# One wait for two tiles: how SyncE issues the count-matrix writes of a graph kernel

## The reference, cut to what matters

```python
h = jnp.maximum(_layernorm(x, axis=-1), 0.0)
x = x + _L0_gnn_ref(h, edge_attr_64, ..., edge_index)   # an MLP for each edge, segment_sum over src
h = jnp.maximum(_layernorm(x, axis=-1), 0.0)
x = x + _L1_gnn_ref(h, W, attn, rel_emb, src, dst, edge_type_100)   # attention, segment_sum over dst
...
x = x + _L2_gnn_ref(h, edge_index, W, b)                # graph convolution, segment_sum(msg, col)
x = x + _L3_gnn_ref(h, edge_index, ...)                 # mean over the neighbours, segment_sum(x[src], dst)
```

## Time and profile before

| | |
|---|---|
| median of 3 runs | 3380.41 us (3377.36 to 3380.56) |
| the profiled execution | 3380.8 us, of which its span in the trace is 3379.1 us |
| mean granted TensorE clock over the span | 0.866 of full speed |
| edge tiles, first to last accumulation | 1330.8 to 2585.7 us from the span's start |
| busy over the span | PE 74%, DVE 77%, POOL 58%, ACT 44% |

### The profile page before, as it was taken

How to read it: one execution, slowest core, us unless ns; L and a number is a source line. 1 busy time by engine, 2 the same in 40 slices (tenths; PEclk the granted TensorE clock), 3 DMA queues, 4 the chain that set the end, 5 groups by cost and what they waited for, 6 DMA issues and landing times. The chain is left out here.

```text
span 3379.1 us, 87741 instructions
## 1 busy us (share of the span) xinstructions
PE 2511.1 (74%) x20390; PEld 1974.6 (58%) x20391; DVE 2597.0 (77%) x8325; ACT 1489.4 (44%) x3942; POOL 1952.3 (58%) x2344
## 2 busy tenths in 40 slices
PE   1433555555555554999999999999999239989899
PEld 1322334333334343999999999999997214445455
DVE  7863777777777773999999999999997779983501
ACT  2011222222222222677777777777775655452200
POOL 1005777777777777899999999999996000000000
PEclk9975677677777776999999999999999559999999
DMA  9993222222222223888888888888886669869766
GB/s 381 414 414 129 78 78 83 78 78 78 77 79 78 78 68 104 236 240 234 242 239 235 240 239 234 242 238 236 241 239 226 255 282 343 301 219 315 249 220 208
DMA packets 738172, 696.84 MB, mean 206 GB/s; under 512 B 48524, under 2 KB 637275, under 8 KB 734779
## 3 DMA queue, kind: packets, MB, share of 16 engines
q1 hardware_dynamic: 516770, 536.77, 47.6%
q10 hardware_dynamic: 195544, 104.71, 12.7%
q0 software_dynamic: 25792, 54.52, 4.9%
HBM read 340.91 MB, written 354.90 MB: 206 GB/s over the span
## 5 line engine op out<-in xcount | busy, mean ns | idle before, releaser
L855 POOL DMA_INDIRECT sorted_rows<-rows,posi x806 | 785.1, 974 | 338.7 <-issue 221.4
L1147 DVE SCALAR_TENSOR_TENSOR acc<-acc,keep,pm 128x256 f32<-128x256 f32 x1504 | 715.7, 476 | 70.9 <-issue 23.9
L965 POOL TENSOR_SCALAR ohs_e<-iota,rt 128x128 f32<-128x128 f32 x1128 | 666.2, 607 | 12.4 <-DMA rt<-sorted_rows 12.4
L803 PE MATMUL s_peq<-sb_w1bb,eT 128*128 128x256 f32 x806 | 352.5, 531 | 398.9 <-ACT eT L658 379.9
L1074 PE MATMUL pm<-ohw_e,ohs_e 128*128 128x128 f32 x3008 | 609.1, 283 | 0.0
L974 POOL TENSOR_TENSOR hid<-pre_e,excess 128x512 f32<-128x512 f32 x376 | 482.8, 1284 | 117.2 <-ACT excess L1001 117.2
L1080 PE MATMUL px<-PN,dT 128*128 x4512 | 498.1, 219 | 0.4 <-ACT dT L1014 0.4
L1020 ACT ACTIVATE ohw_e<-ohd_e,rt 128x128 f32<-128x128 bf16 x1504 | 490.5, 397 | 0.0
L1074 PEld LDWEIGHTS pm<-ohw_e,ohs_e 128*128 128x128 f32 x3008 | 461.8, 194 | 0.0
L803 PEld LDWEIGHTS s_peq<-sb_w1bb,eT 128*128 128x128 f32 x806 | 172.8, 265 | 441.1 <-ACT eT L658 432.7
L1091 PE MATMUL ps<-hid,ohs_e 128*128 128x129 f32 x3008 | 424.3, 283 | 0.5 <-POOL hid L974 0.5
(11 more groups left out here) (317 smaller groups left out, 4206.3 us busy)
## 6 DMA issues: line engine op xcount, KB each, us to landing
count_matrices<-acc SPq DMA_DIRECT2D x1504, 128.0 KB, 2.6
sorted_rows<-zrow SPq DMA_DIRECT2D x188, 528.0 KB, 10.5
rt<-sorted_rows ACTq DMA_DIRECT2D x184, 528.0 KB, 4.6
gab<-count_matrices SPq DMA_DIRECT2D x60, 1280.0 KB, 6.0
arb<-count_matrices SPq DMA_DIRECT2D x25, 1664.0 KB, 8.8
ab<-count_matrices SPq DMA_DIRECT2D x25, 1600.0 KB, 9.3
arb<-count_matrices SPq DMA_DIRECT2D x25, 1536.0 KB, 8.5
ef<-in_edge_attr_dram SPq DMA_DIRECT2D x58, 364.0 KB
```

The lines of the kernel that those rows point to most:

```text
L803: nc.tensor.matmul(pe_q[:, q % 2, 0:2 * D], eT[:, q % 2, :], w1bb[:], start=True, stop=True).then_inc(s_q, 1)
L855: pool.indirect_dma_start(sortd, bass.IndirectOffsetOnAxis(ap=posi[:, h, c:c + 1], axis=0), rows[:, h, c, :], None).then_inc(s_sc[h], 16)
L965: last = nc.gpsimd.tensor_scalar(ohs[:, k % BUFS, j, :], iota128[:], rt[:, k, j, D + 1:D + 2], None, ALU.is_equal)
L1147: nc.vector.scalar_tensor_tensor(acc[:, k % SUMS, j, :], before, keep[:, at:at + 1] if isinstance(at, int) else keep[:, ds(at, 1)], pm[:, ...
```

## The change

SP waits before the first and the third tile of a group only. It waits there until the second or the fourth accumulation is counted, and then issues two writes, one behind the other. What is written, from where, to where and in which order stays the same, and so do the semaphores that the writes add to.

```diff
@@ -941,7 +941,8 @@
                     n = i * RING + k
                     rows = loads(nc, mybir.EngineType.SP, tilei[0:1, 2, ds(n * G, G)], DUMMY + SUMS * G - 1)
                     for j in range(G):
-                        sp.wait_ge(s_acc, n * G + j + 1)
+                        if j % 2 == 0:
+                            sp.wait_ge(s_acc, n * G + j + 2)
                         sp.dma_start(ar[:, ds(rows[j], P, NT), :].rearrange("a p c -> p a c"),
                                      acc[:, k % SUMS, j, :].rearrange("p (a c) -> p a c", a=2)).then_inc(s_w[k % SUMS], 16)
```

## The result

The change makes the kernel slower: 3396.46 us median of 5 runs (3394.81 to 3399.54) against 3377.36 us (3376.14 to 3380.56) for the kernel before, run beside it. The ratio is 1.0056 with a 95% interval of 1.0041 to 1.0071, some 19 us. The profiled execution took 3398.77 us. In the changed kernel the lines from 945 on count one more: the wait is L945, the write L946, the accumulation L1148, the matmuls into `pm` L1074 and L1075.

The account below looks back on a forecast made before the run. No single engine was taken to bound it: PE, DVE and POOL at 99, 94 and 91%, coupled through small buffers. Hidden savings, free delays, moved issues at 0 and 0.1 us gained at the end gave 3380 us, range 3367 to 3395.

Parts of the forecast that it names:

- no difference to tell: Whole kernel: a change under 0.2% (6.8 us), chance 0.50, own range 3374 to 3387 us.
- caught loads: Edge tiles: SP's moved issues hold up one more register load per pass, 14 us slower, 3394 us; chance 0.22.
- SP isn't what limits: Edge tiles: SP's round of 2.93 to 3.16 us stays under the group's 3.34; opposite rival 3328 us, chance 0.03.
- the removed waits: SP, edge tiles: two waits fewer save 0.14 us a group, 53 us in all, but hidden.
- the slots' reserve: Slots of `acc`: later writes leave 2.1 us at the worst, cost nothing; late-slot rival 3399 us, chance 0.03.
- The "issue" idle time: DVE before its accumulations: ready but its sequencer hadn't handed over the instruction; forecast within 22.7 +/- 10 us.
- I see about as many to be freed as to be caught, and take the sum at 0: Edge tiles: register loads newly held by SP's moved issues balance those freed; 0, bounds -25 and +14 us.
- the bound of +14 us: Edge tiles: upper bound for moved issues, one newly held load in each of 47 passes at 0.3 us.
- the hold-up rule: Register loads: an SP issue beginning about 0.3 us after a load's start holds it until the issue ends.
- The test that the prediction set itself: Edge tiles: wrong if the mean group leaves 3.34 us by over 0.02; L62 durations on DVE and PE should then move.
- The wait count: SP, edge tiles: it would wait about twice a group, not 0.7 times, longer in total than 63 us.
- The end of the stage: Edge tiles' end: last issue 0.7 to 0.9 us after the last accumulation, gain 0 to 0.18 us, taken as 0.1.

Follow-up runs that it names:

- experiment 1: Changed kernel with the two removed waits put back on counts already met, pairs kept; 3397.05 us, 1.0050 of the kernel before.
- experiment 5: Kernel before with PE's register load alone replaced by a constant in the edge tiles; 3373.92 us, 0.9980 of the kernel before.
- experiment 6: Changed kernel with PE's register load alone replaced by a constant; 3378.12 us, 0.9994 of the kernel before.
- experiment 9: Changed kernel with only PE's late load, one in eight, right behind its loop's branch, replaced by a constant; 3378.92 us, 1.0002 of the kernel before.
- experiment 10: Kernel before with only PE's late load, one in eight, right behind its loop's branch, replaced by a constant; 3375.50 us, 0.9988 of the kernel before.
- experiment 13: Changed kernel with single waits in groups 3, 4 and 5 of a pass, pairs in the others; 3398.36 us, 1.0052 of the kernel before.
- experiment 17: Changed kernel with the first pair waiting for DVE's addition in group 5 alone; 3397.70 us, 1.0059 of the kernel before.
- experiment 7: Changed kernel with SP's register load moved between a group's two pairs, from an address moved by two; 3531.09 us, 1.0437 of the kernel before.
- experiment 2: Changed kernel with one wait for all four tiles of a group, then four writes; 3395.67 us, 1.0047 of the kernel before.
- experiment 18: Changed kernel with edge-row loads cut to 16 KB in place of 528 KB for two groups; 3398.77 us, 1.0052 of the kernel before.
- experiment 8: Changed kernel with the pairs waiting for three and for four accumulations; 3431.14 us, 1.0158 of the kernel before.
- experiment 11: Changed kernel with PE's register load moved to the head of a step, ahead of `turn`; 3408.97 us, 1.0092 of the kernel before.
- experiment 12: Kernel before, single waits, with DVE's register load moved ahead of its addition; 3430.76 us, 1.0158 of the kernel before.
- experiment 15: Changed kernel, pairs kept, with DVE's register load moved ahead of its addition; 3460.49 us, 1.0231 of the kernel before.
- experiment 16: Changed kernel with each group's first pair waiting for DVE's addition, except in the last two groups; 3408.18 us, 1.0092 of the kernel before.

## Why the prediction was wrong

It gave 3380 us, "no difference to tell", and a range up to 3395. The median is 3396.46, outside by 1.5 us. The rival "caught loads", 3394 us with a chance of 0.22, is the one that came, in direction and nearly in size, but not by the mechanism that it was given.

**What held.** SP isn't what limits, and the removed waits are worth nothing: putting them back changes nothing (experiment 1). A pair's issues are 0.56 us apart (1998.42 to 1998.98) against the forecast 0.55. No accumulation waits for a write, so the slots' reserve was enough. The next tile 0 is issued 1.80 to 1.97 us after E in groups 2 to 5, by the median, where 1.78 was forecast. The "issue" idle time of 21.3 us is within 22.7 +/- 10.

**The step that failed** is "I see about as many to be freed as to be caught, and take the sum at 0". The term measured some +18 us: 17.8 in the stage, 19 between the medians of the whole kernel. Even the bound of +14 us was too low. Three things were wrong in it.

First, it was made from DVE's loads alone. The one load of PE among the rows was used as a witness for DVE's; what PE's loads were worth was never asked. Experiments 5, 6, 9 and 10 put some three quarters of the loss on one PE load in each pass. The eight-group table of the kernel before would have pointed to it: the late load starts 0.45 us behind the others, DVE waits for `pm` once a pass, in the group behind it (0.39 us at 2020.26), and at 333 ns the load was undisturbed.

Second, the balance of freed and caught was a guess over "a few of the eight groups". The trace allowed a count. By the table the kernel before has two groups with clearly long loads on both engines (1 and 3), and in the changed one DVE's load is longer in groups 0, 2 and 4, shorter in 1, 3 and 5; that part indeed nearly cancels, 3.04 us of loads in a pass against 3.07. The cancelling was right for DVE, and PE, with 0.5 us more, was left out. That the rival's price of 14 us comes near the 19 us measured is in part luck: one longer load in each pass is what came, but PE's, and not held by the rule that the price was made from.

Third, the hold-up rule, read from four single loads, doesn't hold. Experiments 13 and 17 have an issue inside the alleged critical distance with a short load, and one outside of it with a long load.

The test that the prediction set itself says the same: the group left 3.34 us by more than 0.02 (0.04 to 0.05), and the durations of L62 did move with it. "DVE's median load still near 310" was wrong, at 376. The wait count was wrong too, once a group, not "about twice". The end of the stage was wrong by sign: 1.38 us, where 0.7 to 0.9 was forecast. In the last groups accumulations follow each other at 0.5 us, and SP's last four issues stand behind a register load that begins only when the pair before is out. It costs 0.5 us.

For a register load the prediction set the floor of about 600 ns of the Trainium skill ("DMA: Bandwidth & Descriptors", section "Latency and other measured facts") against the trace's 310. The shortest load of each engine took 294 to 329 ns in every kernel, SP's moved loads of experiment 7 apart, so the page's figure is no floor here; some 600 ns is what the late load takes when it is disturbed.

**What is shown, and what stays open.** Shown: the loss lies in the edge tiles. It disappears, but for 0.08%, when DVE and PE load no registers. Some three quarters of it go with PE's late load, which takes 619 instead of 333 ns. And it needs the moved issues, not the missing waits. Shown too is what does not stretch the loads by itself: SP's own register load beside them (experiment 2, where it is elsewhere and they are long), an issue that falls on them (13, where they are short), a longer burst of writes (2). Transfers have a part in it: with smaller ones two thirds of the loss between the first pass and the last is gone (18), with the reserve that this kernel has no partner with single waits. Not shown is any share of DVE's loads. Open is what exactly lengthens a load. A load's duration follows the place of the whole sequence in time, and every edit that moved one thing moved others; I know no single neighbour whose distance orders the long and the short loads of all these kernels. No kernel with the computation whole was found that beats the kernel before.

## What to carry to other kernels

A few nanoseconds of bookkeeping moved on an engine with time to spare can cost half a per cent, through small operations of other engines whose duration isn't fixed. Before a moved issue is called free, list such operations (register loads above all) on every engine, by their place in the loop, the round behind the branch too, and price the undisturbed ones as losses to come. To find what a loss goes through, take the suspect out of both kernels and look at the difference of the two ratios, and of the stage alone in the two traces: the time of the whole kernel also holds what the edit costs elsewhere (experiment 18). Moving the suspect elsewhere brings its own costs: kernels 7, 8, 11, 12, 15 and 16 were 0.9 to 4.4% slower than before and hardly told the theories apart.

## What the runs showed of the hardware

- A register load of one number (DVE) or four (SP and PE) takes 294 to 330 ns undisturbed and up to 0.97 us disturbed (experiments 2 and 15). In the changed kernel loads of DVE and PE reach 0.80 us without any change in these engines' own programs. In experiment 12 DVE's median went from 310 to 474 ns by moving the load ahead of one operation.
- In the kernel before only register loads that run while edge rows are being transferred are long: on DVE at most 313 ns in the even groups, a median of 416 in the odd ones (1400 to 2560 us). In the changed kernel others are long too.
- A load of four numbers from an address two numbers off the multiple of four took 1.02 to 1.42 us (experiment 7, 1400 to 2560 us); no load from a multiple of four took more than 0.97 in any kernel.
